# Causal self attention: later keys set to zero in the probabilities by GpSimd instead of masked in the scores by a product

## The reference

```
x = x + _L0_attn_ref(_layernorm(x, axis=-1), L0_attn_w_attn, L0_attn_w_proj)

qkv = x @ w_attn.T                                   # 16 heads of 16
att = jnp.einsum('bhqd,bhkd->bhqk', q, k) / jnp.sqrt(jnp.float32(D))
causal = jnp.tril(jnp.ones((t, t), dtype=bool))
att = jnp.where(causal[None, None], att, -jnp.inf)
att = jax.nn.softmax(att, axis=-1)
y = jnp.einsum('bhqk,bhkd->bhqd', att, v)
return y @ w_proj.T
```

## Time and profile before

| | before |
|---|---|
| median of the runs | 2728.5 us |
| profiled execution, its time | 2728.54 us |
| its span, first to last instruction | 2726.8 us |
| mean granted clock of TensorE | 0.920 |
| busy: PE, DVE, ACT, POOL | 2324.1, 1431.7, 1129.5, 739.8 us |
| causal stage, tiles from first to last | 69 to 505 us |

### The profile page before, as it was taken

How to read it: one execution, slowest core, us unless ns; L and a number is a source line. 1 busy time by engine, 2 the same in 40 slices (tenths; PEclk the granted TensorE clock), 3 DMA queues, 4 the chain that set the end, 5 groups by cost and what they waited for, 6 DMA issues and landing times. The chain is left out here.

```text
span 2726.8 us, 44343 instructions
## 1 busy us (share of the span) xinstructions
PE 2324.1 (85%) x13938; PEld 1449.0 (53%) x13939; DVE 1431.7 (53%) x3865; ACT 1129.5 (41%) x2652; POOL 739.8 (27%) x852
## 2 busy tenths in 40 slices
PE   4999999789954488669999999967778689999998
PEld 2455555445542245323444333334446579999997
DVE  3766666234359235247777777444445643333333
ACT  1665666323311244127777777622222023333332
POOL 3111111132323222133222322033322233333333
PEclk8999999889976689879999999988887699999999
DMA  4232222100010430022222222010003612222221
GB/s 147 83 94 84 81 78 79 34 5 5 3 53 0 70 61 10 18 70 67 66 69 71 71 71 70 15 41 6 9 5 138 249 28 35 35 35 34 38 33 25
DMA packets 134893, 148.73 MB, mean 55 GB/s; under 512 B 25374, under 2 KB 119240, under 8 KB 134600
## 3 DMA queue, kind: packets, MB, share of 16 engines
q1 hardware_dynamic: 121048, 128.83, 15.8%
q0 software_dynamic: 13680, 17.84, 4.1%
HBM read 100.71 MB, written 46.01 MB: 54 GB/s over the span
## 5 line engine op out<-in xcount | busy, mean ns | idle before, releaser
L447 ACT ACTIVATE self_probs<-self_score_ps 128x512 f32<-128x512 f32 (+3 forms) x1024 | 481.1, 516 | 330.9 <-PE self_score_ps L768 169.3
L586 DVE TENSOR_REDUCE self_neg_max<-self_max_ps 128x1 f32<-128x512 f32 x512 | 329.0, 685 | 155.5 <-PE self_max_ps L754 149.6
L754 PE MATMUL self_max_ps<-self_k_stack,self_q_stack 96*128 96x512 bf16 (+3 forms) x1024 | 354.5, 351 | 37.5 <-DVE self_neg_max L583 17.7
L765 PE MATMUL self_score_ps<-self_q_stack,self_k_stack 99*128 99x512 bf16 (+3 forms) x1024 | 344.5, 344 | 1.6 <-ACT self_probs L447 1.6
L2211 ACT ACTIVATE x_stream<-experts_up_ps,experts_bias_now 128x128 f32<-128x128 f32 x568 | 162.0, 368 | 382.2 <-PE experts_up_ps L2432 382.2
L583 DVE CUSTOM_DVE_ANT_0 self_masked<-self_max_ps,self_later 128x128 f32<-128x128 f32 (+3 forms) x512 | 235.0, 488 | 119.3 <-PE self_max_ps L754 108.0
L2432 PEld LDWEIGHTS experts_up_ps<-experts_tileT,x_stream 128*128 128x128 f32 x2272 | 266.9, 193 | 5.2 <-issue 1.6
L2432 PE MATMUL experts_up_ps<-experts_tileT,x_stream 128*128 128x128 f32 x2272 | 267.3, 276 | 1.2 <-DVE x_stream L2348 1.2
L2442 PE MATMUL experts_down_ps<-experts_down,x_stream 128*128 x1136 | 256.8, 379 | 0.0
L779 PE MATMUL self_out_ps<-self_probs,self_values 128*32 128x512 f32 (+3 forms) x2048 | 231.8, 524 | 3.3 <-ACT self_probs L447 1.4
L2442 PEld LDWEIGHTS experts_down_ps<-experts_down,x_stream 128*128 128x128 f32 x1136 | 210.4, 190 | 25.7
(11 more groups left out here) (281 smaller groups left out, 3778.5 us busy)
## 6 DMA issues: line engine op xcount, KB each, us to landing
self_parts_dram<-self_parts SPq DMA_DIRECT2D x64, 384.0 KB, 2.4
self_q_stack<-self_parts_dram SPq DMA_DIRECT2D x384, 64.0 KB, 2.2
self_k_stack<-self_parts_dram SPq DMA_DIRECT2D x384, 64.0 KB, 2.3
experts_up<-moe_up_dram SPq DMA_DIRECT2D x8, 1024.0 KB, 8.3
experts_down<-moe_down_dram SPq DMA_DIRECT2D x8, 1024.0 KB, 10.6
x_stream<-x_dram SPq DMA_DIRECT2D x8, 512.0 KB, 8.3
expert_rows_dram<-experts_down SPq DMA_DIRECT2D x8, 512.0 KB, 6.2
out_dram<-x_stream SPq DMA_DIRECT2D x8, 512.0 KB, 8.5
```

Of the source, the lines that this page charges most:

```text
L447: act.activation(probs[:, i % 8, 0:w], score_ps[:, (16 * n + i) % 3, 0:w], ACT.Exp).then_inc(exp_done, 1)
L586: dve.tensor_reduce(neg_max[:, n % 2, t, h:h + 1], max_ps[:, i % 2, 0:w], AX, ALU.max, negate=True).then_inc(max_read, 1)
L754: last = pe.matmul(max_ps[:, i % 2, 0:w], q_stack[0:ROWS, h, P * t:P * t + P], k_stack[0:ROWS, h, 0:w], start=True, stop=True)
L765: last = pe.matmul(score_ps[:, m % 3, 0:w], k_stack[0:KROWS, head, P * j:P * j + P], q_stack[0:KROWS, head, S - w:S], start=True, stop=not ...
```

## The change

The mask product of the causal case is left out. In its place GpSimd sets the later keys of the diagonal block to zero in the probabilities, after the exponential: one `affine_select` of 128x128 in float32, in place, for every score tile, 16 a group and 512 in all. `with_values` waits for these selects (a new semaphore `later_zeroed`) instead of the exponentials. The selects of a key tile, `zero_later(n, j)`, are placed by hand between the other work of GpSimd. The second self attention is not changed.

```
+                def zero_later(n, j):
+                    if causal:
+                        for h in range(GH):
+                            i = 4 * j + h
+                            pool.wait_ge(exp_done, 16 * n + i + 1)
+                            block = probs[:, i % 8, 0:P]
+                            pool.affine_select(out=block, in_=block, compare_op=ALU.is_ge, fill=0.0, base=0,
+                                               pattern=[[1, P]], channel_multiplier=-1).then_inc(later_zeroed, 1)
...
+                        zero_later(4 * b, 0)
                         third_part(b + 1, 0)
+                        zero_later(4 * b, 1)
...
                         third_part(b + 1, 1)
+                        zero_later(4 * b, 2)
...
+                        zero_later(4 * b, 3)
...
                     cut_shift(4 * b + 2)
+                    zero_later(4 * b + 1, 0)
...
                             inverse_deviation(b + 2)
+                        zero_later(4 * b + 1, 1)
                         third_part(b + 1, 2)
+                        zero_later(4 * b + 1, 2)
                         third_part(b + 1, 3)
...
-                                     q_stack[0:KROWS, head, S - w:S], start=True, stop=not causal)
-                    if causal:
-                        last = pe.matmul(score_ps[:, m % 3, 0:P], c.ident_b[:], c.causal_kq[:], start=False, stop=True)
+                                     q_stack[0:KROWS, head, S - w:S], start=True, stop=True)
...
-                    pe.wait_ge(exp_done, 16 * n + 4 * j + 4)
+                    pe.wait_ge(later_zeroed if causal else exp_done, 16 * n + 4 * j + 4)
```

More of the change, by code:

```diff
@@ L160, in self_attention @@
         shift_placed = [sem(f"shift_placed{g}") for g in range(NG)]
-        score_full, exp_done, pv_done = sem("score_full"), sem("exp_done"), sem("pv_done")
+        score_full, exp_done, later_zeroed, pv_done = sem("score_full"), sem("exp_done"), sem("later_zeroed"), sem("pv_done")
         o_copied, ot_full, sums_inverted, o_done = sem("o_copied"), sem("ot_full"), sem("sums_inverted"), sem("o_done")
@@ L367, in _ @@
                         third_part(b + 1, 1)
+                        zero_later(4 * b, 2)
                         if norm:
                             square(b + 1, 3)
+                        zero_later(4 * b, 3)
+                    else:
+                        for j in range(TT):
+                            zero_later(4 * b, j)
                     cut_shift(4 * b + 2)
+                    zero_later(4 * b + 1, 0)
                     if b + 1 < B:
@@ L376, in _ @@
                             inverse_deviation(b + 2)
+                        zero_later(4 * b + 1, 1)
                         third_part(b + 1, 2)
+                        zero_later(4 * b + 1, 2)
                         third_part(b + 1, 3)
                         add_bias(b + 1)
+                    else:
+                        zero_later(4 * b + 1, 1)
+                        zero_later(4 * b + 1, 2)
+                    zero_later(4 * b + 1, 3)
                     cut_shift(4 * b + 3)
+                    for j in range(TT):
+                        zero_later(4 * b + 2, j)
                     if b + 1 < B:
@@ L385, in _ @@
                         square(b + 2, 1)
+                    for j in range(TT):
+                        zero_later(4 * b + 3, j)
             @block.scalar
```

## The result

The changed kernel takes 2735.3 us (median of nine runs, 2733.0 to 2741.6) against 2728.2 us of the kernel before in the same comparison: ratio 1.0031, 95% interval 1.002 to 1.0041. It is slower by 0.3%, where a gain of 3.1 us was forecast. The profiled execution has a span of 2732.7 us.

What follows compares the result with a forecast made beforehand. TensorE was taken to bound the causal self attention. Seven batches at 0.40 us save 2.8, the last batch 0.5 less 0.3, the start 0.1: 3.1 in total, so 2728.5 - 3.1 = 2725.4 us, range 2717 to 2736.

Steps and rivals of the forecast that it cites:

- The masks: TensorE in the causal stage: 30 of 64 mask products a batch lost in waits, 34 come out, saving 1.97 us.
- The selects: GpSimd, 64 a batch: 0.26 us each, 16.6 us a batch, hidden under TensorE.
- The stall: First group of batches 0 to 6: TensorE's product of key tile 1 waits 1.57 us for GpSimd's third part and selects.
- Seven batches at 1.97 - 1.57 = 0.40 us: Causal stage, all but the last batch: masks saved less stall gives 0.40 us a batch, 2.8 us saved.
- the rivals: Selects at 0.34 us (2727.6 us, 0.20); fewer masks lost (2719 or 2713, 0.15); slower queue (2737, 0.16); no stall (2714, 0.04).
- the slower rival: GpSimd's in-order queue bounds the second group's first two key tiles; selects at 0.55 us, 8.5 us slower, 2737 us; chance 0.16.
- Seven of the eight batches look like that one: Causal stage: seven batches were taken to be like the one worked out, which takes 56.67 us.
- the 2.8 of the sum: Causal stage: 2.8 us saved by seven batches at 0.40 us each.
- nothing behind the stall gives time back: Behind the product of key tile 1, the next wait begins with a chain TensorE itself feeds, so the 1.57 us stays lost.

Runs made afterwards that it cites:

- the two halves of the split: Two runs of the kernel before, without selects: one without the 30 masks counted as lost, 2726.3 us; one without the other 34, 2709.8 us.
- the wait filled: The changed kernel with 13 useless score products on TensorE ahead of the waiting product of key tile 1, first group, batches 0 to 6: 2725.7 us.

## Why the prediction was wrong

- **The masks** were right: 34 of 64 a batch come out. 1.97 us was worked out, 1.98 measured, and the two halves of the split confirm it, 0.0 and 1.98.
- **The selects** were right: 0.25 us apart and 292 ns each, close to the 0.26 and 282 ns of the rows of before.
- **The stall** was right: 1.57 us worked out, 1.51 and 1.45 measured.
- **The step that failed** is "Seven batches at 1.97 - 1.57 = 0.40 us". It takes the granted clock of 1.00 of the earlier trace rows as given behind the stall, and so puts the fall of the clock at nothing without a reason, though the change adds an idle stretch to TensorE. Behind six of the seven stalls the clock fell to half for 3.4 us, while TensorE was full of work, and each fall cost 57.75 - 56.13 = 1.6 us. In the trace the five falls behind the first batch cost 8.2 us. The first batch took 56.2 us against 52.6 with the wait filled; 1.7 of these 3.6 us came behind its stall, and 1.9 ahead of it, from the longer half-clock stretch with which the stage began. So the falls are 9.9 of the 12.3 us by which the stage ends later in the one trace than in the other (525.1 and 512.8 us), and over the runs the two kernels are 9.6 us apart. None of the rivals had it.
- The measured 2735.3 us lies just inside the range of 2717 to 2736 us and near the 2737 of the slower rival. Both are luck. That rival, GpSimd's queue as the bound of the second group, did not happen; it takes selects of twice the length.
- "Seven of the eight batches look like that one" was a misreading that mattered little: before the change five take 56.66 us, the first 52.8 and the seventh 53.7. With the wait filled the first saves 0.15 us, the five 0.53 each and the seventh 0.46, together 3.3 for the 2.8 of the sum.
- The prediction's sentence that nothing behind the stall gives time back was right, but it did not ask whether something behind it would take more.
- Left open: what exactly about the stretch decides whether the clock falls. In two traces it fell behind 12 of 14 stalls of 1.38 us without masks. In one trace each, it fell behind four of seven with 4 useless products in them, behind none with 13, and behind none of 1.43 us with masks. No run isolates which feature of TensorE's work around the stall counts. Nor was it tried why the first batch began with a longer half-clock stretch in some traces (to 77.9 us here, to 72.0 before). The stall does not bring it about, for the stretch begins ahead of it, at 67.7 us, and it lasted to 75.0 in the run without the 34 masks, which has no selects at all.

## What to carry to other kernels

When work moves to an engine with room on average, look at what stands ahead of it in that engine's queue: here one call in the wrong place cost 20 us, and the 512 added instructions nothing in a full batch. Before an instruction is taken out of a busy TensorE, follow at each of its waits the chain on the other engine back to where TensorE feeds it; what lies between is not a gain. And where a change puts a new idle stretch into a stage that ran at the full clock, price the fall of the clock behind it, at the cost of what stands there: here 1.6 us each time.

## What the hardware showed that was not expected

A stall of 1.4 us in a stage that is otherwise full was in most batches followed by 3.4 us at half clock. 13 useless products in each of the seven stalls made the kernel 9.6 us faster. The four float32 projection products behind the stall took 1.88 us at the full clock and 3.57 at half. VectorE's reductions were not slowed by the selects beside them: one of 512 columns took 686 ns with selects and without, and the batch is 54.68 us with selects and 54.67 without.
